# A graph network on one core: layer 1's edge scores, with the looked-up columns laid out score by score instead of block by block

## The reference, cut to what matters

```python
xl = x @ W_lin + b_lin
s_i = xl @ W_att[:hc]            # (n, 4)
s_j = xl @ W_att[hc:]            # (n, 4)
alpha = s_i[row] + s_j[col] + b_att
alpha = jnp.where(alpha >= 0, alpha, 0.2 * alpha)
```

## Time and profile before

| | us |
|---|---|
| median of 3 runs | 6518.53 (6496.33 to 6520.01) |
| the profiled execution | 6552.88 |
| its span in the profile | 6551.1 |

### The profile page before, as it was taken

One profiled execution on the slowest core, in us unless ns is written; L12 is line 12 of the kernel. 1 busy time (PEld: TensorE's weight loads), 2 busy tenths in 40 slices (PEclk: granted clock), 3 DMA queues, 4 the chain that ended last, 5 costly groups with the idle time before them and its releaser, 6 DMA issues.

```text
span 6551.1 us, 75285 instructions
## 1 busy us (share of the span) xinstructions
PE 3121.8 (48%) x17770; PEld 2320.0 (35%) x17776; DVE 2909.3 (44%) x6787; ACT 799.6 (12%) x3180; POOL 3256.4 (50%) x3682
## 2 busy tenths in 40 slices
PE   4111335665455512732344565656895455553333
PEld 3111234655333302722333222224654233352333
DVE  6222685222344412872333565668514454782111
ACT  1000110000000001000000243335500000251000
POOL 3666204666566675006666355554414566105665
PEclk9999999999666655555556777777997666785556
DMA  1000012111211101422223222333426777661112
GB/s 50 21 22 22 14 53 57 45 44 45 27 23 22 23 2 24 116 53 63 68 70 65 63 89 87 94 83 102 122 69 198 255 258 258 204 214 48 46 45 48
DMA packets 297618, 525.97 MB, mean 80 GB/s; under 512 B 83307, under 2 KB 166497, under 8 KB 290785
## 3 DMA queue, kind: packets, MB, share of 16 engines
q0 software_dynamic: 119584, 235.61, 15.3%
q1 hardware_dynamic: 177960, 289.53, 14.2%
HBM read 423.29 MB, written 101.61 MB: 80 GB/s over the span
## 4 chain that ended last, share of the span: by engine, by line
another core or an unknown queue 23%; DVE 23%; issue 22%; PE 19%; POOL 6%; DVEq 3%; ACT 2%; DMA 1%; SPq 0%; POOLq 0%; ACTq 0%; PEldq 0%
PE ps L2106 5%; POOL work L814 5%; PE ps L2445 3%; PE ps L2405 2%; DVE acc L1629 2%; PE ps L2105 2%; DVE acc L1557 2%; DVE work L1307 1%; PE ps L2373 1%; PE ps L2125 1%; DVE alpha L1331 1%; DVE aS L1691 1%; ACT work L1995 1%; PE ps L2179 1%
## 5 line engine op out<-in xcount | busy, mean ns | idle before, releaser
L814 POOL DMA_INDIRECT work<-t_h,idx_slot x832 | 794.8, 955 | 855.4 <-DMA t_h<-acc 309.4
L814 POOL DMA_INDIRECT work<-t_v,idx_slot x832 | 793.9, 954 | 434.0 <-issue 231.1
L2106 PE MATMUL ps<-work 128*128 128x128 f32 (+1 forms) x2496 | 663.1, 408 | 583.7 <-issue 299.7
L2106 PEld LDWEIGHTS ps<-work 128*128 128x128 f32 x2496 | 540.9, 295 | 645.4 <-issue 644.8
L2373 PE MATMUL ps<-big,work 128*128 x832 | 463.0, 711 | 278.6 <-DVE acc L1557 127.8
L814 POOL DMA_INDIRECT work<-t_xl,idx_slot x416 | 424.6, 1021 | 196.6 <-issue 110.6
L2445 PE MATMUL ps<-big,work 128*128 x832 | 335.0, 556 | 320.1 <-issue 166.1
L773 POOL DMA_INDIRECT rec_by_src<-sc_rec_s,sc_idx x392 | 380.6, 971 | 114.0 <-issue 109.3
L2061 PE MATMUL ps<-work 128*128 128x25 bf16 x800 | 76.9, 184 | 636.4 <-DVE work L1052 503.6
L2445 PEld LDWEIGHTS ps<-big,work 128*128 128x128 f32 x832 | 211.9, 276 | 443.2 <-issue 407.6
L814 POOL DMA_INDIRECT work<-t_kv,idx_slot x208 | 199.3, 958 | 333.8 <-DMA t_kv<-big 174.5
(11 more groups left out here) (504 smaller groups left out, 6982.8 us busy)
## 6 DMA issues: line engine op xcount, KB each, us to landing
work<-rows_of_v_by_position SPq DMA_DIRECT2D x52, 1024.0 KB
work<-relT_by_dst SPq DMA_DIRECT2D x156, 256.0 KB
rows_of_h_by_position<-work SPq DMA_DIRECT2D x52, 512.0 KB
work<-rows_of_h_by_position SPq DMA_DIRECT2D x52, 512.0 KB
rows_of_v_by_position<-work SPq DMA_DIRECT2D x26, 1024.0 KB
rows_of_v_by_position<-acc SPq DMA_DIRECT2D x26, 1024.0 KB
work<-t_v,idx_slot POOLq DMA_INDIRECT x832
work<-relT_by_src SPq DMA_DIRECT2D x52, 256.0 KB
```

Of the source, the lines that this page charges most:

```text
L814: nc.gpsimd.indirect_dma_start(to, None, table, bass.IndirectOffsetOnAxis(ap=idx_slot[:, h * HU + k:h * HU + k + 1], axis=0)).then_inc(s_g ...
L2106: ins = M.matmul(psum_blocks[:, ds(b, 1), 0:width], oh[:, s, :], ring[:, h * HU + k, 0:width].unsqueeze(1), start=False, stop=False)
```

## The change

Score and block change places in the layout. The moving operand of the wide matmuls is read as score, then block: `node12[:, :, c, :]` with `p b f -> p f b`. It is still 100 columns of the same numbers, but now each column lies 24 bytes from the one before, where until now four neighbours (8 bytes) were read before each step. In PSUM each tile's 104 columns are four scores of 26 blocks; the wide matmuls write 25 of each 26, and the narrow ones write one column at each of the four places left, 26 columns apart. The number of matmuls stays.

The multiply is split in two, one for each PSUM bank, since its patterns have one dimension more. The mask is read in runs of 26. The sum over blocks reads `pick1` in neighbouring columns, where it read every fourth.

```diff
-                two = pick1.rearrange("p (c z f) -> p c z f", c=2, f=4)
-                hi = ohhi1[:, s, :].rearrange("p (c z) -> p c z", c=2)
-                V.tensor_tensor(two, ps[:, 2 * s:2 * s + 2, 0:416].rearrange("p c (z f) -> p c z f", f=4),
-                                bc(hi, 4), ALU.mult).then_inc(ph("L1_picked"), 1)
+                hi = ohhi1[:, s, :].rearrange("p (k b) -> p k b", b=26)
+                for c in (0, 1):
+                    four = slice(4 * c, 4 * c + 4)
+                    last = V.tensor_tensor(pick1.rearrange("p (k f b) -> p k f b", f=4, b=26)[:, four, :, :],
+                                           ps[:, 2 * s + c, 0:416].rearrange("p (k f b) -> p k f b", f=4, b=26),
+                                           hi[:, four, :].unsqueeze(2).to_broadcast([P, 4, 4, 26]), ALU.mult)
+                last.then_inc(ph("L1_picked"), 1)
                 dve.wait_ge(ph("L1_picked"), m + 3)
-                V.tensor_reduce(alpha[:, tiles_of(i, h), :], pick1.rearrange("p (k b f) -> p k f b", b=26, f=4), AX,
+                V.tensor_reduce(alpha[:, tiles_of(i, h), :], pick1.rearrange("p (k f b) -> p k f b", f=4, b=26), AX,
                                 ALU.add).then_inc(ph("L1_scored"), 1)
```

```diff
                     for c in range(3):
-                        M.matmul(ps[:, bank, at:at + 100].rearrange("p (b f) -> p b f", f=4), ohTd[:, s, k * P:(k + 1) * P],
-                                 node12[:, :, c, :], start=c == 0, stop=c == 2)
+                        M.matmul(ps[:, bank, at:at + 104].rearrange("p (f b) -> p f b", b=26)[:, :, 0:NB], ohTd[:, s, k * P:(k + 1) * P],
+                                 node12[:, :, c, :].rearrange("p b f -> p f b"), start=c == 0, stop=c == 2)
                     for c in range(3):
-                        last = M.matmul(ps[:, bank, at + 100:at + 104].rearrange("p (b c f) -> p b c f", b=1, c=1), ohTr[:, s, k * P:(k + 1) * P],
+                        last = M.matmul(ps[:, bank, at:at + 104].rearrange("p (f b) -> p f b", b=26)[:, :, NB:26].rearrange("p f b -> p b f").unsqueeze(2), ohTr[:, s, k * P:(k + 1) * P],
                                         node11[:, ds(blocks[k], 1), c:c + 1, :], start=c == 0, stop=c == 2)
```

## The result

Twenty executions each: 6501.52 us before (median; 6450.26 to 6530.76), 6537.49 after (6510.72 to 6567.39). The ratio is 1.0062, 95% interval 1.0047 to 1.0077: 31 to 50 us slower. The forecast was 60 us slower. Its 6579 stood on a median of 6518.5, that of the three executions known then, so 6579 and 6537.5 can't be set against each other directly. Against the 40 us of the ratio the direction was right and the size half as large again as it should be.

A forecast was written before the change was run, and what follows sets the result against it. DVE was taken to set the stage's pace before, PE after: 0.9 + 52 x 5.59 (290.7) + 2.3 = 293.9 us against 233.6, 60 more, so 6518.5 + 60 = 6579 us; range 6486 to 6625.

The forecast's parts named there:

- above DVE's new 3.9, so PE sets the pace and DVE waits for it: In the stage, PE would need 5.59 us a half against DVE's 3.9, so PE runs without idle.
- The price of a wide matmul: On PE, 100 columns each read alone would take 188 ns instead of 83.
- 1.78 ns a column from DVE's stepped sum: Alternative column price from DVE's sum over every fourth word; it would give a stage of 281 us, kernel 6566.
- 1.88: Chosen price in ns of a column read alone, from `count`'s stepped weight load: 60 ns over 32 elements.
- the second reading: In `count`, the 25 moving columns set the 60 ns: 2.4 ns a column, kernel 6644; 8 in 100 for nearer 2.4.
- share the other 0.135, 45 ns each: On PE, a tile's three narrow matmuls take 0.135 us before the change, and were counted the same after it.
- DVE's part: Sum 0.61 us shorter at 1.02, two multiplies of 0.59 costing 0.07 more as a pair: 0.54 us saved a half.
- The first rival: Stepped read costs the matmul nothing; DVE sets 3.9 us a half, kernel 28 us less, 6490; 15 in 100.
- 1.2 us a half is all that PE may lose: In the stage, DVE needs about 4.4 us a half, PE 3.1 to 3.2, before PE becomes the slower one.
- The second rival: Clock rises to 2.4 GHz in the stage; narrow matmuls fall to about 26 ns, stage 37 us more, 6556; 22 in 100.

The follow-up runs named there:

- the read alone: Kernel before, with only the wide matmuls' read order changed to score, then block, writing back to the old places; stage 262.4 us.
- the table by score: Changed kernel plus a copied table, so wide matmuls read adjacent columns; stage 230.9 us, ratio to before 1.0016; repeated on the third chip 230.6 us, 0.9994.

## Why the prediction was right, and where it was not

**The mechanism is shown.** The forecast's step "above DVE's new 3.9, so PE sets the pace and DVE waits for it" is what the profile after has, and the read alone does it (262.4 us), while undoing the read alone takes it away (230.9 us). The direction of the forecast rests on this.

**The price of a wide matmul** was taken as 188 ns and is 181, within 4%; of the readings, 1.78 ns a column from DVE's stepped sum was nearest. That 1.88 came so close is in part luck. It was worked out from `count`'s weights, as 32 to each of four lanes, and called a cycle of 1.2 GHz at 0.83 ns; but the granted clock was 1.00 in both stretches of `count` (below), and no run here tests the four lanes.

```profile
12.00:69.00 57.00, 53.22 (x801) 50.74 (x801) 44.25 (x103) 18.50 (x49) 0.00 (x0) 1.00 0.29 75
758.00:828.00 70.00, 30.82 (x806) 25.73 (x805) 68.45 (x100) 19.82 (x52) 0.00 (x0) 1.00 0.05 14
```

25 moving columns at the 1.81 ns measured here would be 45 ns of `count`'s 60, so the 2.4 ns of the second reading was not the moving columns' price. In this stage 7 ns too many over 1248 of them are 9 us.

**The term that was mis-sized is the three narrow matmuls, "share the other 0.135, 45 ns each".** I read 45 ns as their own price and carried it over. About 18 of them were the price of TensorE's queue at the old pace, and they cost 27 or 28 once wide matmuls are slow. 0.135 - 0.084 = 0.051 us a tile, x 416 = 21 us. The two together are the 30 us by which the stage (+30.6) missed the forecast (+60). The fetch of the block numbers, which the prediction didn't count, costs nothing in the changed kernel: at 2703.9 to 2704.9 it runs beside the half's last matmuls, the last of which starts at 2704.99.

**DVE's part** was right to a hundredth: 1.02 us for the sum, 0.586 each for the multiplies, the pair 1.09. As forecast, it was spent on waiting, only with 57 us and not 85, since PE was quicker than counted.

**The first rival fell, and its number would have been wrong too.** Stepped reads are charged. But without the charge the kernel would not have gained 28 us: the step "1.2 us a half is all that PE may lose" took PE's idle for slack. The profile put it down to DVE (69.4 of 80 us), since the one-hots came last, yet the fetch of the block numbers took nearly as long. In the gap of the earlier trace rows, after the last narrow matmul at 2709.93 and before the wide one at 2711.33, TensorE's queue has two loads and then its semaphore instruction (first and last start at the end of each row):

```profile
L477 PEldq TENSOR_LOAD <-block_of_tile_s x2: 330/330/331, 2710.1 to 2710.5; - x2
L2223 PEldq EVENT_SEMAPHORE  x1: 51/51/51, 2711.1 to 2711.1; - x1
```

Over the 51 gaps of the kernel before, the median is 1.39 us from the last narrow matmul's start to the next wide one's, and 1.18 of it had passed when the queue was ready. So about 0.2 us a half was slack, not 1.2. With a faster DVE the same gap reads "issue", and a half with three narrow matmuls a tile can't go below 4.32 us: 2.7 us of gain for the stage instead of 28.

**The second rival** (the clock rises) did not come about: 0.50 in the stage, PE without idle. Where the clock did rise, in the read alone, a tile went from 0.626 to 0.620 us, which is 2.5 us over 416 tiles and not the 23 I gave it; the narrow matmuls had come down already without it. The nearness of its 6556 to the result is an accident.

**What stays open** is the clock itself, and by how much the next limit behind the queue, the transfers, is GpSimd's doing. Why the clock stood at 0.94 to 0.99 in some of these runs and at 0.50 in others with nearly the same work was not tried.

## What to carry to other kernels

A layout that pleases the engine that reads last may be paid for by the engine that reads or writes first, as here; before changing it, look for one row in the trace with the same step in bytes on the other engine, as `count` had. Two elements on each 16 bytes are nearly enough for a matmul's moving operand, so the table, which is copied once, is the thing to lay out anew, not its access pattern. And before counting on an engine's idle time, ask what its queue does in it: an idle put down to another engine may hide a fetch of almost the same length, which comes out only when the other engine gets faster.

## What the runs showed of the hardware that was not expected

- A bf16 column of the moving operand that is alone on its 16 bytes takes 1.8 ns, at a granted clock of 0.50 (181 and 179 ns for 100 columns) as at 0.99 (181). Two on each 16 bytes take 95 ns for 100, where adjacent ones take 85.
- A column that is written alone to PSUM takes two cycles: 86 ns for 100 at a clock of 1.00, 167 at 0.50. Adjacent columns take 45 to 46 at 1.00 and 84 at 0.50, and runs of 25 take 85 at 0.50. So a stepped write at the full clock looks like an ordinary matmul at half clock.
- With a register instruction of 46 ns in the queue for each, the small matmuls took 41 to 46 ns instead of 27, at the low clock; where the matmuls before them took 181 ns they were back at 27.
- The kernel before took 6559 us on one chip and 5195 on another. The stage looked at here, in the table by score, took 230.9 us on the first and 230.6 on a third (5193 us), although GpSimd worked beside it for 131 us on the third and not at all on the first.
